# Vision tower kernel: gx's last sum on VectorE, the feed-forward slots of ScalarE rearranged, the class token's energy written per group

## What is computed

```python
h = hypot(sobel_x(x), sobel_y(x)).sum(axis=channel)       # x: 16 images, 3 channels, 256 x 256
h = concat([cls_tok, h])                                  # 16 x 257 tokens x 256, a row is a token
y = layernorm(h)
idx = top_k(norm(y, axis=-1), 27)                         # the 27 tokens of most energy of each image
q = y[idx] @ Wq.T + bq;  k = y @ Wk.T + bk;  v = y @ Wv.T + bv      # 16 heads of 16
r = broadcast(mean(y, axis=1));  r[idx] = softmax(q k.T / 4) v @ out_w.T + out_b
h = h + r
z = layernorm(h)
g = quant8(z) @ ternary(w1).T                             # 1024 hidden channels
g = silu(depthwise_conv_3(g) + conv_b)
out = h + quant8(g) @ ternary(w2).T
```

## Times and profile before

| | us |
|---|---|
| median of 3 runs | 1550.82 |
| lowest and highest | 1550.23, 1552.83 |
| the profiled execution | 1551.41 |
| its span, first to last instruction | 1549.6 |
| VectorE busy in it | 1319.3 |

### The profile page before, as it was taken

One profiled execution on the slowest core, in us unless ns is written; L12 is line 12 of the kernel. 1 busy time (PEld: TensorE's weight loads), 2 busy tenths in 40 slices (PEclk: granted clock), 3 DMA queues, 4 the chain that ended last, 5 costly groups with the idle time before them and its releaser, 6 DMA issues.

```text
span 1549.6 us, 11187 instructions
## 1 busy us (share of the span) xinstructions
PE 819.3 (53%) x3334; PEld 647.0 (42%) x3334; DVE 1319.3 (85%) x2024; ACT 718.5 (46%) x1294; POOL 167.4 (11%) x208
## 2 busy tenths in 40 slices
PE   3465100467647733556648643456648633586534
PEld 1233000345546522445537533345537532475423
DVE  7999998898996999998997899998998799522576
ACT  2212242255486534255475644156476544243662
POOL 0000000022313000012303000012303000000000
PEclk8787555757679876667679876567579876688876
DMA  8000600034717510125618510116527010100001
GB/s 201 3 11 14 116 0 0 1 60 76 120 25 127 103 41 0 28 48 89 103 33 133 106 41 1 28 31 105 92 44 130 7 41 1 28 1 1 0 0 27
DMA packets 46356, 78.13 MB, mean 50 GB/s; under 512 B 7466, under 2 KB 31706, under 8 KB 44634
## 3 DMA queue, kind: packets, MB, share of 16 engines
q0 software_dynamic: 33408, 50.34, 20.0%
q1 hardware_dynamic: 12314, 26.31, 7.4%
q10 hardware_dynamic: 576, 0.79, 0.2%
HBM read 22.84 MB, written 4.25 MB: 17 GB/s over the span
## 4 chain that ended last, share of the span: by engine, by line
DVE 45%; ACT 14%; PE 13%; issue 8%; DMA 5%; POOL 0%; SPq 0%; DVEq 0%; ACTq 0%
DVE arena L564 15%; DVE arena L567 13%; ACT arena L1376 3%; DVE arena L953 3%; PE psum L1717 2%; PE psum L1811 2%; DMA arena<-nrows_mem 2%; DMA arena<-zT 2%; ACT arena L1249 2%; PE psum L1833 1%; DMA arena<-img 1%; DVE red L580 1%; ACT arena L1513 1%; PE psum L1786 1%; PE psum L1729 1%
## 5 line engine op out<-in xcount | busy, mean ns | idle before, releaser
L564 DVE TENSOR_TENSOR arena<-arena 128x768 f32<-128x768 f32 (+2 forms) x519 | 475.9, 968 | 58.2 <-ACT arena L1291 50.8
L567 DVE SCALAR_TENSOR_TENSOR arena<-arena 128x768 f32<-128x768 f32 (+2 forms) x224 | 201.5, 949 | 0.1
L1729 PE MATMUL psum<-zT,w1q 128*128 128x257 f32 x512 | 138.8, 405 | 21.0 <-DVE gpad L948 16.0
L1729 PEld LDWEIGHTS psum<-zT,w1q 128*128 128x128 f32 x512 | 103.0, 204 | 43.4 <-DVE gpad L948 20.9
L1717 PE MATMUL psum<-gpad,win 128*128 128x257 f32 x288 | 78.3, 411 | 47.8 <-ACT gpad L1388 47.8
L1833 PE MATMUL psum<-arena 128*128 128x257 f32 x128 | 55.0, 604 | 90.5 <-ACT arena L1491 72.1
L540 POOL DMA_DIRECT2D h<-others x60 | 51.5, 859 | 436.6 <-DVE others L567 357.0
L1328 ACT ACTIVATE arena<-arena 128x768 f32<-128x768 int16 x32 | 27.0, 844 | 154.1 <-DVE arena L567 153.7
L1717 PEld LDWEIGHTS psum<-gpad,win 128*128 128x128 f32 x288 | 57.4, 205 | 63.7 <-ACT gpad L1388 53.8
L1249 ACT ACTIVATE arena<-arena 128x256 f32<-128x256 f32 x65 | 23.3, 409 | 127.2 <-DVE arena L567 68.2
L1833 PEld LDWEIGHTS psum<-arena 128*128 128x128 f32 x128 | 36.8, 301 | 102.5 <-ACT arena L1491 75.8
(11 more groups left out here) (235 smaller groups left out, 2109.6 us busy)
## 6 DMA issues: line engine op xcount, KB each, us to landing
arena<-nrows_mem POOLq DMA_DIRECT2D x36, 384.0 KB, 7.7
arena<-img POOLq DMA_DIRECT2D x36, 384.0 KB, 7.6
img<-x SPq DMA_DIRECT2D x36, 258.0 KB, 7.0
h<-others POOLq DMA_DIRECT2D x60, 128.0 KB, 2.7
arena<-arena POOLq DMA_DIRECT2D x18, 384.0 KB, 8.8
arena<-zT POOLq DMA_DIRECT2D x12, 384.0 KB, 8.4
out<-out SPq DMA_DIRECT2D x16, 256.0 KB
img<-x SPq DMA_DIRECT2D x48, 64.5 KB, 6.7
```

The costliest lines, as they stand in the source:

```text
L564: return v.tensor_tensor(o, a, b, op)
L567: return v.scalar_tensor_tensor(out=o, in0=a, scalar=s, in1=b, op0=op0, op1=op1)
L1729: ins = mm((A0, A1, B0, B1)[i % 4][:, 0:S], w1q[:, k, t * P:(t + 1) * P], zT[:, k, b, :], start=(k == 0), stop=(k == DT - 1))
```

## The change

Four things are changed.

1. The third sum of gx is no longer a DMA. GpSimd's two DMAs of `nrows` into `tmp[f][1]` of each pair go; VectorE subtracts the image row itself, between slots -2 and -1 of pairs 1 to 3, when the two other sums have landed, and signals `gx_ready`. ScalarE's absolute value of gx waits for that. Three rounds, three pairs, two rows: 18 DMAs go, 18 subtractions of 128x768 come.
2. `nrows` is then needed by gy alone: ScalarE makes it in slot 2 of pairs 0 to 2, and the copies in slot 6 go.
3. `FFN_SLOTS` becomes a list of single pieces of work (s: scale, t: take, a: SiLU), with scales and takes taking turns, and with other slots. Nothing stands any more in slots -2 to 0 of pair 3, and all four SiLUs are inside the pairs. In pair 1 VectorE's `context(1)`, `shares(2)`, `queries(3)` go from slot 0 to slot 1.
4. The class token's energy is read back into `topk` in each group, ahead of that group's other energies, and `select` waits for both.

```diff
 FFN_SLOTS = (
-    {2: ((0, 1, 2, 3), None, ()), 3: ((4, 5), None, (0, 1)), 4: ((6,), None, (2, 3)), 5: ((7,), None, (4, 5)),
...
-    {-2: ((), None, (14, 15)), -1: ((), 1, ()),
...
+    {1: "s13 t10 s14 t11 s15 t12 s16 t13 s17 t14 s18 t15 a1", 3: "t16 s19 t17 s20 t18 s21 t19 s22",
...
-    GX_SUMS = 48
-    NEG_ROWS = 8
+    GX_SUMS = 32
+    NEG_ROWS = 6
...
-                    sp.dma_start(topk[:, 0, 0:1], ec_dram.to_broadcast([GB, 1])).then_inc(erow_in, 16)
 
                 sp.wait_ge(e_ready, g + 1)
+                sp.dma_start(topk[:, 0, 0:1], ec_dram.to_broadcast([GB, 1])).then_inc(erow_in, 16)
                 sp.dma_start(e_dram, e9[:, 0:ROWS]).then_inc(e_out, 16)
...
-                for f in range(2):
-                    pool.wait_ge(gx_sums[f], at_x + 32)
-                    pool.wait_ge(neg_rows, negs + 2 * i + f + 1)
-                    pool.dma_start(tmp[f][1], nrows[:, f], accum_op=ALU.add).then_inc(gx_sums[f], 16)
...
                     slot(-2)
+                    for f in F:
+                        dve.wait_ge(gx_sums[f], ((g - 1) * (PAIRS - 1) + i - 1) * GX_SUMS + 32)
+                        tt(tmp[f][1], tmp[f][1], px(2 * i + f + 2, 2), ALU.subtract).then_inc(gx_ready, 1)
                     slot(-1)
...
-                dve.wait_ge(erow_in, g * 16 + 32)
+                dve.wait_ge(erow_in, g * 32 + 32)
...
-                    if k == 0:
+                    if k == 1:
                         context(step, g, 1)
                         shares(step, g, 2)
                         queries(step, g, 3)
...
                         a = tmp[f][1]
-                        act.wait_ge(gx_sums[f], g * (GX_SUMS * (PAIRS - 1)) - GX_SUMS * (PAIRS - 1 - i))
+                        act.wait_ge(gx_ready, n2 - 2 * PAIRS + f + 1)
                     s.activation(a, a, ACT.Abs).then_inc(mags, 1)
...
-                    if k == 2 and i == 0:
+                    if k == 2 and i < PAIRS - 1:
                         for f in F:
                             s.activation(nrows[:, f], img[:, :, 2 * i + f + 2, 2:2 + W], ACT.Copy, scale=-1.0).then_inc(neg_rows, 1)
...
-                    if k == 6 and i < PAIRS - 1:
-                        for f in F:
-                            act.wait_ge(gy_sums[f], g * (48 * (PAIRS - 1)) - 48 * (PAIRS - 1 - i) + 16)
-                            s.activation(nrows[:, f], img[:, :, 2 * i + f + 4, 2:2 + W], ACT.Copy, scale=-1.0).then_inc(neg_rows, 1)
...
-                ffn_take(gl, (), GB - 1, ())
```

More of the change, by code:

```diff
@@ L38 @@
 FFN_SLOTS = (
[6 rows of a table removed]
+    {2: "s0 s1 s2 s3", 3: "t0 s4 t1 s5 t2 s6", 4: "t3 s7", 6: "t4 s8 t5 s9 t6 s10", 7: "t7 s11 a0", 8: "t8 s12 t9"},
+    {1: "s13 t10 s14 t11 s15 t12 s16 t13 s17 t14 s18 t15 a1", 3: "t16 s19 t17 s20 t18 s21 t19 s22",
+     6: "t20 s23 t21 s24 t22 s25",
+     7: "t23 a2 s26 t24 s27 t25 s28 t26 s29 t27 s30 t28 s31 t29 t30 t31 a3"})
 TILE_SLOTS = tuple((2 * k, 2 * k + 1) for k in range(8)) + ((),)
@@ L1286, in magnitude_rows @@
                         a = tmp[f][0]
-                        act.wait_ge(gx_ready, g * 2 - 1 + f)
+                        act.wait_ge(gx_ready, n2 - 2 * PAIRS + f + 1)
                     else:
                         a = tmp[f][1]
-                        act.wait_ge(gx_sums[f], g * (GX_SUMS * (PAIRS - 1)) - GX_SUMS * (PAIRS - 1 - i))
+                        act.wait_ge(gx_ready, n2 - 2 * PAIRS + f + 1)
                     s.activation(a, a, ACT.Abs).then_inc(mags, 1)
                 def with_carry(k):
-                    if k == 2 and i == 0:
+                    if k == 2 and i < PAIRS - 1:
                         for f in F:
@@ L1379, in silu, with ffn_take @@
                 s.activation(idle[:, half:half + 1], clsT[:, 0:1], ACT.Copy)
-            def ffn_take(gf, scale, image, take):
+            def ffn_take(gf, work):
                 nt = gf * (GB * FT)
-                for i in scale:
-                    if i >= 4:
-                        act.wait_ge(conv_psum, nt + i - 3)
-                    act.wait_ge(g_psum, nt + i + 1)
-                    s.activation(gpad[:, i % 4, 1:S + 1], (A0, A1, B0, B1)[i % 4][:, 0:S], ACT.Copy).then_inc(gd_ready, 1)
-                if image is not None:
-                    act.wait_ge(conv_taken, nt + (image + 1) * FT)
-                    silu(gf, image, image % 2)
-                for i in take:
-                    t = i % FT
-                    act.wait_ge(conv_psum, nt + i + 1)
-                    s.activation(ydw[:, t, :], (C0, C1, T0, T1)[i % 4][:, 0:S], ACT.Identity,
-                                 bias=cb[:, t:t + 1]).then_inc(conv_taken, 1)
+                for what, i in [(w[0], int(w[1:])) for w in work.split()]:
+                    t = i % FT
+                    if what == "s":
+                        if i >= 4:
+                            act.wait_ge(conv_psum, nt + i - 3)
+                        act.wait_ge(g_psum, nt + i + 1)
+                        s.activation(gpad[:, i % 4, 1:S + 1], (A0, A1, B0, B1)[i % 4][:, 0:S], ACT.Copy).then_inc(gd_ready, 1)
+                    elif what == "t":
+                        act.wait_ge(conv_psum, nt + i + 1)
+                        s.activation(ydw[:, t, :], (C0, C1, T0, T1)[i % 4][:, 0:S], ACT.Identity,
+                                     bias=cb[:, t:t + 1]).then_inc(conv_taken, 1)
+                    else:
+                        act.wait_ge(conv_taken, nt + (i + 1) * FT)
+                        silu(gf, i, i % 2)
             def tap_diagonals(tiles):
@@ L1574, in slot @@
                     if k in FFN_SLOTS[0]:
-                        ffn_take(g, *FFN_SLOTS[0][k])
+                        ffn_take(g, FFN_SLOTS[0][k])
                 return slot
@@ L1580, in slot @@
                     if k in FFN_SLOTS[1]:
-                        ffn_take(g, *FFN_SLOTS[1][k])
+                        ffn_take(g, FFN_SLOTS[1][k])
                 return slot
```

## The result

| | before | changed |
|---|---|---|
| median, us | 1551.59 (4 runs) | 1525.74 (4 runs) |
| lowest and highest | 1550.23, 1552.83 | 1524.22, 1527.63 |
| the profiled execution | 1551.41 | 1525.84 |
| its span | 1549.6 | 1524.0 |

The ratio is 0.9834, 95% interval 0.9817 to 0.9851: 25.9 us faster, where 40.6 were forecast (1510.2, range 1503 to 1523). The direction was right, the size was not, and the time lies outside the range.

The account below looks back on a forecast made before the run. VectorE bounds the kernel, busy 1319.3 of 1549.6 us, so its waits and work set the time. Terms sum to -13.6 us a round, -40.8 for three, +0.2 once: 1550.82 - 40.6 = 1510.2 us, range 1503 to 1523.

Parts of the forecast that it names:

- The wait of pair 3: VectorE's first maximum in pair 3: its 16.1 us wait for gx's absolute values becomes 0.1; pair 3 forecast -15.3 us a round.
- Pair 1: Pair 1: 4.6 us wait for picked heads goes, new 2.1 us wait for absolute values; with the subtractions -0.8 us a round.
- Pair 2: Pair 2: two subtractions cost 1.74 us on VectorE, the rest of the DMA waits saves 0.8; +0.9 us a round.
- The fourth SiLU: End of pair 3: ScalarE's fourth SiLU comes late for VectorE's fourth reduction, +1.5 us a round, between 0 and +4.
- The slow restart: TensorE ahead of the fourth SiLU: first convolution 2.94 not 1.57 us after the pause, some 2 us in all, SiLU 3 late.
- the nearer of two rows: TensorE's pause before the fourth SiLU taken as nearer 3.59 us idle (convolution 1.57) than 7.34 idle (2.94).
- The last part: From the last group's energies to the end: readback 0.3 us later, +0.2 us once, between 0 and 1.
- the row sums did meet the image load: Rival: image load slows or starves pair 2's row sums; starved, 1 to 3 us a round, 1513 to 1519; chance 0.12.
- Slot 1 of pair 3: Slot 1, scales, takes and second SiLU: needs 14.4 us, room 15.4, so it fits with 1 us to spare.
- slot 3: Slot 3 of pair 3: a new table load of 1.28 us fills 1.46 us idle; +0.2 us a round, between 0 and 1.3.
- The clock did not stay low through pair 3: Rival: TensorE's clock stays at 1.2 GHz through pair 3, +26 us a round, 1583 us; chance 0.04.
- the 4 us estimated from it: Rule against the change: 1.38 us drain per table switch makes slot 3 1.4 us dearer a round, time 4 us longer.

Follow-up runs that it names:

- The run with gx alone: Kernel before with gx's subtractions on VectorE, nrows copies in slot 2 and class token's energy per group, but old slots and context in slot 0: 1560.91 us, ratio 1.0072.
- the run with the slots alone: Changed kernel with gx's third sum back as a DMA and the old wait and nrows copies; new slots, later context and class token stay: 1518.03 us, ratio 0.9783.
- The first experiment: Changed kernel, but in pair 2 VectorE's two subtractions of gx stand behind the output offsets instead of ahead: 1515.54 us, ratio 0.9768.
- the second experiment: Changed kernel, but in slot 7 of pair 3 scales 26 and 27 stand ahead of the third SiLU: 1515.49 us, ratio 0.9771.
- the kernel before with two operations: Kernel before with two more 128x768 operations on VectorE (about 1.9 us) ahead of the last group's select: 1556.19 us, ratio 1.0029.

## Why the prediction was wrong

- **The wait of pair 3** was read right: -15.0 us a round, -15.3 forecast. The run with gx alone keeps it and the run with the slots alone loses it, so it was the slots that took it away.
- **Pair 1** was right: -0.7 against -0.8 (a wait of 2.13 us for the absolute values, 2.1 forecast).
- **Pair 2 is the first step that failed.** I costed the two subtractions as 1.74 us of VectorE's own time and asked only what waits for them in VectorE's program. Behind them stood the output offsets, for which TensorE's residual matmuls, ScalarE's residual sums, and through these VectorE itself wait in the same pair. That gave +2.6 a round and not +0.9: 5.0 us in all. The first experiment gives the 1.7 us a round back by changing the order alone.
- **The fourth SiLU is the second**, a term that was mis-sized: +3.3 a round and not +1.5, 5.5 us in all. The slow restart was among the bounds (3 late), but I let the nearer of two rows choose: the one with a pause of 3.59 us and no slow start. The pause was 5.03 us, since TensorE had run ahead of ScalarE by then (its last g before the pause ended as the third SiLU began), and the restart was slow: 13.0 us from scale 26 to the fourth SiLU and not 10.5. Pauses of 2.28 us (in the second experiment) and 2.20 us (in slot 3 of the change, then 2.84 us for six matmuls) were followed by slow starts too, so picking the row by the pause's length was the mistake.
- **The last part is the third**: +4.0 and not +0.2. I took it for a constant, since the change doesn't touch it. Some 0.5 lies ahead of the first MAX8, where the token's DMA is (inside its bound of 1). The other 3.4 us (224.2 and 220.8 us) come with TensorE's clock: TensorE is busy 3 us longer in that stretch, VectorE and ScalarE are not. In the twelve profiles the same stretch spans 5.5 us. What sets the clock there stays open. No bound of mine had that.
- The three together are 14.3 us (5.0, 5.5 and 3.8) of the 15.0 us that the profiled execution is off, and the next largest is 0.8 us of pair 3. Each alone, and any two of them, would have left the time in the range.
- **Of the rivals**, the row sums did meet the image load, and harder than I took as likely: 10.75 us for one of them (the load was issued at 495.3 us and its packets ran from 496.3 to 518.0, not from 493 to 513 as I had it),

```profile
512.66 0.86 POOL L534 DMA_DIRECT2D h<-others  x1 [10.75 <-DMA h<-others]
...
518.99 0.10 POOL L518 MEMSET rowmark<- 128x1 f32 x1 [5.47 <-DMA h<-others]
```

  but the second row was done at 519.0 and VectorE asked for it at 523.7, so it cost nothing; 5 us are left of its cover. Slot 1 of pair 3 fitted with 0.82 us to spare (1 forecast), and slot 3 cost 0.4 to 0.5 us a round (0.2 forecast). The clock did not stay low through pair 3: it was 0.50 to 0.58 from 490 to 505 us and 1.00 from 505 to 515. The table loads of 1.28 us had no drain behind them in the change either: one starts at 533.98 and its SiLU at 535.27. The Trainium skill ("ScalarE: Activation LUTs", "What ACT_TABLE_LOAD costs") puts such a drain on each switch of set; the trace doesn't agree, and the 4 us estimated from it are not what was missing.

Left open: what sets TensorE's clock in the last part, why the later subtractions also shorten pair 3 and the stretch behind it by 1.1 us a round, and where pair 1's 2.3 us of the second round with gx alone come from. The last need not be the subtractions: 2.6 us of the same kind came up in the first round of the kernel before with two operations, whose rounds are unchanged.

## What to carry to other kernels

When an instruction is put into an engine's program, the price is not its own length but that of everything behind it that another engine hands back within the same stage: follow each successor out and back before calling the place free. When a wait is removed by moving work to the end of a stage, look at who feeds that end; two small copies ahead of a long SiLU were worth 10 us, since they give the feeding engine work during it. And a part that a change doesn't touch may still differ by some microseconds with the granted clock, from kernel to kernel and from execution to execution (here 5.5 us in 220): for a change below half a per cent compare stretches of the profile, and not only totals.

## What the runs showed of the hardware

- TensorE's granted clock after a pause can't be told from the pause's length alone: eight equal matmuls took 3.79 us behind 2.96 us of idle time (granted clock 0.50) and 2.00 us behind 3.33 (1.00). The same 616 matmuls or so took between 218.8 and 224.3 us with all that hangs on them, and 1.9 us of work more made one kernel 5.3 us slower and another 3.0 us faster.
- An adding DMA of 128 KB between two on-chip buffers took 10.75 us to the next step while an image load filled the DMA engines, and 2.10 us in the third round, which has no load: five times as long. It did not have to wait for the load's end, which came at 518.0 us, 5 us behind the next step. But its first packet came only 7 us behind its issue at 501.06 us. The queues in the change (packets, MB, share of 16 engines), from 501.1 to 508 us and then from 508 to 511.4:

```profile
q1 hardware_dynamic: 411, 1.46, 106.2%
```

```profile
q1 hardware_dynamic: 198, 0.59, 81.9%
q0 software_dynamic: 144, 0.13, 24.8%
```

  The Trainium skill ("DMA: Bandwidth & Descriptors", "Queues, rings and completion order") lets the DMA engines take turns packet by packet. The second stretch agrees, as both queues moved data in it; it does not say why the first 7 us passed without a packet of the sum, and the trace doesn't either.
- A write of 4 KB was confirmed 1.41 to 1.44 us after its issue in 41 cases, and 2.33 to 2.57 us after it in the seven in which an 8 KB transfer of the instruction queue started while its packets or those of the DMA of 4 elements ahead of it still ran. That DMA of 4 elements cost the write 0.3 us, its own issue, and no more where no such transfer fell in.
